# Mamba-style scan with a mixing layer: B products of two pairs in one GpSimd operation, and a fourth C product on GpSimd in every third step

## What is computed

```python
def step(state, inp):
    d, b, c, u = inp
    dA = jnp.exp(d[..., None] * A)
    state = state * dA + (d * u)[..., None] * b[:, None, :]
    y = jnp.einsum('bdn,bn->bd', state, c)
    return (state, y)
...
y = y + D[None, :, None] * x
y = y * silu(z)                       # z: layer norm of the input
```

## Time and profile before

| what | value |
|---|---|
| time, median of 3 runs | 506.48 us (505.49 to 507.95) |
| profiled execution: its own time | 505.38 us |
| profiled execution: span | 503.4 us |
| VectorE busy | 473.0 us |
| GpSimd busy | 458.0 us |
| TensorE busy | 418.0 us |
| ScalarE busy | 343.3 us |
| mean granted TensorE clock | 0.946 |

### The profile page before, as it was taken

The page is one execution under the profiler, slowest core; times in us unless marked ns, Lnnn a source line. Parts: engine busy times, 40 slices in busy tenths (PEclk is TensorE's granted clock), DMA queues, the critical chain, the costliest instruction groups (busy, mean ns, idle before and its releaser), DMA issues.

```text
span 503.4 us, 4008 instructions
## 1 busy us (share of the span) xinstructions
PE 418.0 (83%) x996; PEld 173.2 (34%) x996; DVE 473.0 (94%) x378; ACT 343.3 (68%) x611; POOL 458.0 (91%) x239
## 2 busy tenths in 40 slices
PE   8748679687859968989898788879988969898897
PEld 5212233233324332434333243324433423343342
DVE  4899999999999999999999999998999979999885
ACT  2787645967469768897688776788788495753321
POOL 1279999999999999999999999989999979999955
PEclk9969989998978989999899899989999989998999
DMA  5799642438990000100891000000593000000002
GB/s 184 265 380 329 156 86 63 88 63 201 274 409 35 0 0 1 63 1 16 306 371 43 0 22 1 21 1 0 182 405 129 0 21 21 23 4 17 21 1 83
DMA packets 17871, 53.96 MB, mean 107 GB/s; under 512 B 2724, under 2 KB 3236, under 8 KB 16824
## 3 DMA queue, kind: packets, MB, share of 16 engines
q1 hardware_dynamic: 16696, 45.31, 24.8%
q0 software_dynamic: 1152, 8.39, 8.2%
HBM read 49.24 MB, written 4.46 MB: 107 GB/s over the span
## 4 chain that ended last, share of the span: by engine, by line
DVE 39%; issue 19%; PE 17%; POOL 12%; ACT 11%; DMA 1%; DVEq 0%; POOLq 0%; SPq 0%; ACTq 0%
DVE dA L860 18%; PE y L463 8%; POOL h L987 7%; DVE h L866 6%; DVE h L860 6%; ACT dA L692 3%; POOL h L980 3%; DVE acc L817 3%; PE work L456 3%; ACT gate L594 2%; PE work L441 2%; PE work L392 1%; DVE work L837 1%; DVE work L831 1%; PE work L433 1%
## 5 line engine op out<-in xcount | busy, mean ns | idle before, releaser
L987 POOL TENSOR_TENSOR h<-b_rep,dtu 128x1024 f32<-128x1024 f32 x127 | 304.1, 2451 | 12.2 <-DVE dtu L945 9.7
L463 PE MATMUL y<-h,ident 128*128 128x512 f32 x512 | 253.7, 632 | 41.4 <-DVE h L866 39.4
L692 ACT ACTIVATE dA<-dt,a_neg 128x512 f32<-128x512 f32 x256 | 165.8, 680 | 98.1 <-DVE h L866 86.4
L860 DVE TENSOR_TENSOR_SCAN dA<-dA,h 128x1024 f32<-128x1024 f32 x79 | 180.6, 2286 | 1.8 <-ACT dA L692 1.8
L463 PEld LDWEIGHTS y<-h,ident 128*128 128x128 f32 x512 | 97.6, 200 | 182.3 <-issue 110.4
L980 POOL TENSOR_TENSOR h<-h,c_rep 128x1024 f32<-128x1024 f32 x49 | 120.3, 2457 | 9.5 <-DVE h L860 9.5
L860 DVE TENSOR_TENSOR_SCAN h<-dA,h 128x1024 f32<-128x1024 f32 x49 | 111.7, 2281 | 7.0 <-ACT dA L692 7.0
L866 DVE TENSOR_TENSOR h<-dA,c_rep 128x1024 f32<-128x1024 f32 x79 | 96.1, 1217 | 0.9
L384 PE MATMUL work<-ctx_sb,w_in 128*128 128x512 f32 x60 | 31.5, 653 | 9.7 <-DVE x L880 9.3
L817 DVE SCALAR_TENSOR_TENSOR acc<-work,chan,acc 128x511 f32<-128x511 f32 (+2 forms) x45 | 32.5, 729 | 5.6 <-ACT acc L573 5.4
L406 PE MATMUL work<-ident,yg 128*128 128x128 f32 x60 | 10.8, 309 | 25.7 <-DVE yg L874 25.7
(11 more groups left out here) (122 smaller groups left out, 385.0 us busy)
## 6 DMA issues: line engine op xcount, KB each, us to landing
b_rep<-bc_scratch SPq DMA_DIRECT2D x32, 512.0 KB, 9.2
c_rep<-bc_scratch SPq DMA_DIRECT2D x32, 512.0 KB, 9.1
fsum<-factors POOLq DMA_DIRECT2D x8, 1024.0 KB, 8.1
x<-x SPq DMA_DIRECT2D x4, 1024.0 KB, 8.7
out<-x SPq DMA_DIRECT2D x16, 256.0 KB, 2.0
ctx_sb<-ctxT SPq DMA_DIRECT2D x3, 512.0 KB, 3.9
ctx_sb<-ctxT SPq DMA_DIRECT2D x2, 256.0 KB, 3.8
w_in<-w_inT SPq DMA_DIRECT2D x1, 384.0 KB, 4.7
```

The source lines that it names most:

```text
L463: mm = pe.matmul(y[:], ident[:], h[:, (s * PAIRS + j) % H_RING, i, :], start=False, stop=(j == SUM_ORDER[-1] and i == 1))
L692: act.activation(dA[:, j % 2, i, :], dt[:, k % 2, :], ACT.Exp, scale=a_neg[:, k, 2 * j + i:2 * j + i + 1]).then_inc(exp_done, 1)
L860: dve.tensor_tensor_scan(pair if on_pool(s * PAIRS + j) else decay, decay, pair, 0.0, ALU.mult, ALU.add).then_inc(scanned, 1)
L987: pool.tensor_tensor(h[:, (s * PAIRS + j) % H_RING], b_rep[:, j], dtu[:, k % 2, :].unsqueeze(1).to_broadcast([P, 2, L]), ALU.mult).then_in ...
```

## The change

In steps 1 to 15 the B products of pairs j - 1 and j (j odd) are one GpSimd operation of 128 x 2048, issued in slot j (`times_b_wide`); it waits for both `b_rep` tiles and both sums. The order in slot j is otherwise kept. Step 0 is as before. In steps 2, 5, 8, 11 and 14 (`is_wide`), GpSimd also makes the C product of pair 6, three slots later, which is slot 1 of the next step, behind the first wide B product there; the order of the sums in these steps ends with 7, 6 instead of 6, 7.

```diff
@@ -56,8 +56,10 @@
 POOL_C = (0, 2, 4)
+WIDE_POOL_C = (0, 2, 4, 6)
 LAST_POOL_C = (0, 2, 4, 5)
 SUM_ORDER = (1, 0, 3, 2, 5, 4, 6, 7)
+WIDE_SUM_ORDER = (1, 0, 3, 2, 5, 4, 7, 6)
 LAST_SUM_ORDER = (1, 0, 3, 2, 4, 6, 5, 7)
@@ -235,9 +237,18 @@
+        def is_wide(s):
+
+            return s % 3 == 2
+
         def on_pool(p):
 
-            return p % PAIRS in (LAST_POOL_C if p // PAIRS == STEPS - 1 else POOL_C)
+            s, j = divmod(p, PAIRS)
+            return j in (LAST_POOL_C if s == STEPS - 1 else WIDE_POOL_C if is_wide(s) else POOL_C)
+
+        def sum_order(s):
+
+            return LAST_SUM_ORDER if s == STEPS - 1 else WIDE_SUM_ORDER if is_wide(s) else SUM_ORDER
@@ -988,6 +999,16 @@
+            def times_b_wide(b, s, k, j):
+
+                pool.wait_ge(b_landed[j], (b + 1) * 16)
+                pool.wait_ge(b_landed[j + 1], (b + 1) * 16)
+                p = s * PAIRS + j
+                pool.wait_ge(summed, max(sums_to_free(p - H_RING), sums_to_free(p + 1 - H_RING)))
+                pool.tensor_tensor(h[:, bass.ds(j, 2)].rearrange("p r i l -> p (r i) l"),
+                                   b_rep[:, bass.ds(j, 2)].rearrange("p r i l -> p (r i) l"),
+                                   dtu[:, k % 2, :].unsqueeze(1).to_broadcast([P, 4, L]), ALU.mult).then_inc(mulb, 2)
+
@@ -1045,7 +1066,9 @@
-                    if p > 0:
+                    if s > 0 and j % 2 == 1:
+                        times_b_wide(b, s, k, j - 1)
+                    if s == 0 and p > 0:
                         times_b(b, s, k, j)
                     if p >= C_LAG and on_pool(p - C_LAG):
                         times_c(p - C_LAG)
```

More of the change, by code:

```diff
@@ L257, in sums_to_free @@
         def sums_to_free(p):
-            return p // PAIRS * PAIRS + SUM_ORDER.index(p % PAIRS) + 1
+            return p // PAIRS * PAIRS + sum_order(p // PAIRS).index(p % PAIRS) + 1
         def dt_bank(n):
@@ L463, in state_sum @@
                     mm = pe.matmul(y[:], ident[:], h[:, (s * PAIRS + j) % H_RING, i, :], start=False,
-                                   stop=(j == SUM_ORDER[-1] and i == 1))
+                                   stop=(j == sum_order(s)[-1] and i == 1))
                 mm.then_inc(summed, 1)
@@ L482, in step @@
                 pe.matmul(y[:], diag_d[:, k, :], u[:, b % 2, k, :], start=True, stop=False).then_inc(y_init, 1)
-                for i, j in enumerate(SUM_ORDER if s < STEPS - 1 else LAST_SUM_ORDER):
+                for i, j in enumerate(sum_order(s)):
                     state_sum(s, j)
```

## The result

The changed kernel takes 513.54 us (median of 4 runs, 510.61 to 515.15), the kernel before in the same comparison 506.75. The ratio is 1.012, with a 95% interval of 1.0087 to 1.0153. So the change makes the kernel 1.0 to 1.2% slower: the direction was forecast, the size, 509.1 with a range to 511.6, was not. All ratios leave out executions more than 1.5% above the fastest of the same kernel; of the kernels here this bears only on "The layer ahead of the late sum".

A forecast was written before the change was run, and what follows sets the result against it. VectorE was taken to set the pace, with GpSimd without slack through steps 1 to 8. The terms +3.1 - 1.1 + 0.6 gave +2.6 us on 506.48, so 509.1 us, range 504.0 to 511.6.

The forecast's parts named there:

- the mechanism up to step 6: Steps 1 to 6: GpSimd has no slack, its queue delays VectorE's scans, with scan (6, 0) 1.0 us later.
- The late sum: End of step 5: pair 6's sum comes last, the next layer starts 3.1 us later, scan (6, 4) is 3.1 later.
- step 8 to 9: VectorE saves 1.1 us in step 8 and keeps it, with no wait at scan (9, 0).
- step 11 to 12: 1.1 us won, then lost as the layer starts 2.6 later than before; counted as +0.6 in the sum.
- What a merge saves GpSimd: Each merge of two B products saves 0.15 us of fixed cost; the wide product takes 4.5 us.
- What GpSimd pays: Up to step 6, 21 merges save 3.15 us, one moved C product adds 2.31; scan (6, 0) comes 1.0 later.
- Step 14 to 15: The move of step 14 wins nothing, only lengthening VectorE's wait before the gating to over 3 us.
- Rival (c): In steps 1 to 15, merging saves GpSimd nothing, 3.2 us more, total 512.2 us; chance 0.1.

The follow-up runs named there:

- The layer ahead of the late sum: The changed kernel with the next step's layer placed ahead of the last two sums in the wide steps: 512.56 us over ten runs, ratio 1.0067.
- Only the moves: The changed kernel with single B products, pair 6's C product still moved in steps 2, 5, 8, 11, 14: 514.93 us, ratio 1.0154.
- the factor's DMA: The changed kernel with the factor's DMA issued behind the wide B product of its slot in steps 1 to 3: 512.72 us, ratio 1.0094.
- three cures at once: The changed kernel with moves in steps 2, 5, 8 only, factor's DMA behind the wide product, step 6's layer ahead of step 5's last two sums: 507.85 us, ratio 1.0021.
- one move: The kernel before with pair 6's C product moved to GpSimd in step 8 alone, single B products: 506.2 us, ratio 0.9978.
- again: The changed kernel measured a second time with no edit: 512.58 us against 507.38 for the kernel before, ratio 1.0097.
- moves in 2, 5 and 8 only: The changed kernel without the moved C products of steps 11 and 14: 509.68 us, ratio 1.0044.
- only the wide products: The changed kernel with wide B products but no C product moved: 508.17 us against 507.38 for the kernel before, ratio 1.0003.

## Why the prediction was right and wrong

**Right: the mechanism up to step 6, and the direction.** VectorE waits for GpSimd at scans (1, 0), (4, 0) and (6, 0): 1.00, 0.38 and 1.50 us, where I wrote 0.6, 0.3 and 1.5, and also at (3, 0), (3, 6) and (5, 6), 0.84, 0.49 and 0.53. The late sum adds 2.1 us between (6, 0) and (6, 4), as written (3.1 - 1.0). "Only the moves" and "the factor's DMA" show GpSimd's queue as the cause of the first, "three cures at once" the place of the layer as that of the second: with the layer ahead, (6, 4) is 0.2 over (6, 0) instead of 2.1.

**Right: step 8 to 9.** Won 1.13 and kept; "one move" measured it alone.

**Right: step 11 to 12.** 1.27 won at (11, 7), 1.7 lost by (12, 4): +0.5, against the 0.6 of the sum.

**Wrong by 2.0 us: "What a merge saves GpSimd" and "What GpSimd pays".** These terms made scan (6, 0) +1.0; it measured +3.05, and +2.8 in "again". The fixed cost of 0.15 us from the earlier trace rows was not what a merge gave. In steps 4 and 5, without DMAs, GpSimd's time from first product to first product fell by 0.31 and 0.32 us for four merges each, 0.08 a merge. The first products of steps 4, 5 and 6, in the changed kernel, then of steps 4 and 5 before (step 6: 198.65):

```profile
141.58 9.14 POOL L1008 TENSOR_TENSOR h<-b_rep,dtu 128x2048 f32<-128x2048 f32 x2
...
168.29 4.61 POOL L1008 TENSOR_TENSOR h<-b_rep,dtu 128x2048 f32<-128x2048 f32 x1
...
199.90 4.59 POOL L1008 TENSOR_TENSOR h<-b_rep,dtu 128x2048 f32<-128x2048 f32 x1
```

```profile
139.70 2.39 POOL L987 TENSOR_TENSOR h<-b_rep,dtu 128x1024 f32<-128x1024 f32 x1
...
166.72 4.72 POOL L987 TENSOR_TENSOR h<-b_rep,dtu 128x1024 f32<-128x1024 f32 x2
```

Over all 21 merges it is 0.11 each ((1.15 + 1.2) / 21), so 0.8 of the missing 2.0 us is the merge. The other 1.2 is that the sum had a DMA moved ahead of the first product without its idle time, 0.40 us three times: no row before had a DMA behind a memset. With the DMA behind the wide product, 0.9 of it went. The figure of the Trainium skill ("GPSIMD Engine Reference", Performance versus the Vector engine), 4,497 ns for 2,048 elements, is near what a wide product takes from start to start up to step 6 (4.51 to 4.60); by that figure the merge would have saved more than my rows said, and it saved less.

**Wrong: "Step 14 to 15" and the tail.** I wrote that the move of step 14 wins nothing and costs nothing, and that VectorE would be idle over 3 us before the gating of step 14; it was idle 0.72 us (2.47 in "again"). The extra product stood in GpSimd's queue: scan (15, 6) waits 2.35 us for GpSimd, TensorE 2.64 for pair 4's product, and the last gating 2.0 more:

```profile
491.96 3.29 PE L474 MATMUL y<-h,ident 128*128 128x512 f32 x4 [2.64 <-POOL h L991]
```

I had not looked at the lead there: before, scan (15, 6) stood at 481.76, 3.4 us behind the end of its own B product but only 1.1 behind that of pair 7 (480.69), which the wide product now has to make too. So it takes the move and the merge together: with either alone VectorE doesn't wait there. From scan (14, 6) to the last gating the shift grows by 1.1 to 2.9 us in the seven traces with a move in step 14 (2.9 and 1.1 in the two of the changed kernel), and by nothing in those of "moves in 2, 5 and 8 only", "only the wide products" and "three cures". Leaving out the moves of steps 11 and 14 is worth 3 to 4 us in the total.

**Not priced: TensorE's clock.** 1.3 us at (10, 3) and 1.7 at (13, 0), in both traces of the changed kernel, and part of the last gating. The kernel before had such sums too, which I had read as ordinary ones:

```profile
388.24 3.56 PE L463 MATMUL y<-h,ident 128*128 128x512 f32 x4 [2.22 <-DVE h L866]
...
455.53 3.05 PE L463 MATMUL y<-h,ident 128*128 128x512 f32 x4 [2.60 <-DVE h L866]
```

The first stands early in step 12, where the scans didn't get later by it; in the changed kernel the sum there takes 1.98 us, and the slow one comes later in the step, close to the layer. The mean granted clock of "again" is 0.946, the same as before. So, as far as these traces show, the change didn't bring a lower clock but slow sums at worse places.

Rival (c), that merging saves nothing, gave 512.2, the nearest of the four numbers, by luck: two thirds of its 3.2 us did come at (6, 0), but 1.2 of them were the DMA's idle time, and merging did save 0.08 to 0.11 us each.

So the profiled execution's sum went: 3.05 instead of 1.0 at (6, 0), 2.1 and -1.1 as written, +0.5 for +0.6 at step 12, 2.6 of clock by (13, 0) (3.0 less what ScalarE's slack in step 11 took back), -1.7 from step 13 to the gating of step 14, where the kernel before had its own slow sum, then 2.5 at (15, 6) and 2.1 at the last gating, part of it clock again (0.62 and 0.52 granted from 492 to 496). That is the 10 us between the two traces; the medians hold 5 to 7 of it. How many sums fall to the lower clock in an execution that wasn't profiled stays open.

## What to carry to other kernels

When work moves to an engine with spare time, ask two things of the place: how far ahead of its reader that engine is there, and what stands behind the moved result in its reader's queue. A product that is ready in time for its direct reader can still hold back work queued behind the sum. Five moves cost 5 to 7 us with the merges and 7.5 without; one of them alone, where GpSimd was itself waiting and ScalarE had 2 us, won about 1. And merging operations on an engine shortens its queue a little, but delays the first of them; alone it changed nothing here that the totals show, since nobody waited for the last.

## What the hardware showed that I had not expected

A DMA that GpSimd issued right behind a memset was preceded by 0.40 us of idle time, three times out of three; issued behind a product it had none. TensorE's granted clock was 0.50 behind idle stretches of about 2 us in some places and stayed at 1.00 behind equal ones in others: the same sum of step 9 followed 1.98 us of idle time in both kernels, and took 1.99 us before and 3.68 after. With 1.9 to 2.3 us of matmuls of zeros in such stretches it stayed at 1.00 at all four places tried; but at each of them the sum took 2.0 us without zeros as well in some traces.
